# A gated convolution and mixture-of-experts block: one group's partial rows summed by accumulating DMAs, and three steps of the order moved

## The chip, the cores and the metric

One core of one Trainium2 chip. The metric is the time of one execution on the device in microseconds (us); before the change it is 213.32 us, the median of 3 runs (213.16 to 214.17). TensorE does the matrix products, VectorE, ScalarE (ACT) and GpSimd (POOL) the rest, SP issues most of the transfers.

## The reference, cut to what matters

The input is `x` (16 batches of 128 channels by 256 positions) and a context of the same shape. The first half is a gated long convolution with 16 heads of 8 channels: the products of all pairs of context channels of a head are convolved along the positions with the head's filter, multiplied with the normalised rows of `x` and summed over one of the two channel indices. The second half is a mixture of experts.

```
kv  = einsum('bhil,bhjl->bijhl', k, v)          # k = v = context
y   = irfft(rfft(kv) * rfft(ssm_kernel))[:L] + kv * D
att = einsum('bijhl,bhil->bjhl', y, layernorm(x))
x   = x + tanh(g_xattn) * att
t   = layernorm(x)
probs = softmax(t @ Wg); e = argmax(probs)      # at most 256 tokens of an expert
x   = x + tanh(g_ffn) * (gate * (silu(t @ W1[e]) * (t @ W3[e])) @ W2[e]
                         + (silu(t @ sw1) * (t @ sw3)) @ sw2)
```

All of it is fp32. The sum over `i` in the third line is what the change touches: eight products for each output row have to be added.

## The kernel before, in words

The 16 batches are worked in four groups of four (g = 0 to 3, the first to the fourth), each group in eight units of two heads, so that the convolution has 32 units or slots s = 0 to 31. From slot 16 on the feed-forward work of the shared expert is interleaved, further slots without a unit follow, and then come the eight routed experts. The order on every engine is written out by hand: `STEPS` and its exceptions `FIRST_STEPS`, `THIRD_STEPS` and `LAST_STEPS` (lines 86 to 97) place each step, and `due` (line 103) reads them: for a group g the slot is 8 (g + 1) plus the step (in the last group 32 plus the step).

One unit runs like this. GpSimd (`kv_products`, lines 503 to 511) multiplies context planes with each other, for four heads at a time, in two instructions of 768 and 128 elements per partition, and ACT makes the squares (`squares`). TensorE (`convolve`, line 1209) multiplies them with the Toeplitz matrices of the two heads into a pair of PSUM banks `z` (three places up to slot 14, then two, because the third goes to the feed-forward). VectorE (`products`, line 968, with `multiply`, line 519) multiplies the result with the turned rows `qr` in six instructions and writes eight rows of terms to the SBUF tensor `terms`, which has eight rows of 24 heads of 64 numbers (`TERMS`, `HEADS`, `TROW`); even groups use the lower 16 heads and odd groups the upper 16. An odd group works units 4 to 7 ahead of 0 to 3 (`unit`, line 122). The semaphore `prods` counts the units that VectorE has finished.

When a group has its eight units, TensorE turns and sums the terms in two halves, `turn_r(g, 0)` and `turn_r(g, 1)` (line 1249): an accumulating transpose for each row of terms, in four blocks of 128 by 128. `FULL_TERMS = 2` says that in groups 0 and 1 all eight rows are summed so, 32 transposes in a half. In groups 2 and 3 GpSimd first adds the upper four rows to the lower four, unit by unit (`fold`, line 676), and TensorE sums four rows, 16 transposes in a half. VectorE adds each half to `x_sb` (`first_residual`, line 977) and takes the statistics of the second layer norm, GpSimd raises them to the power -1/2 (`scale_and_bias`, line 645), ACT normalises into `xrow` (`norm2`), TensorE turns that (`turn_xT`), ACT copies it rounded (`xT_high`) and VectorE writes what the rounding left out (`turned_low`, the step `tokens_low`). The first feed-forward product of a group needs both (`wait_xT`, line 1275). In group 0 `turn_xT` stands in slot 15 and `tokens_low` in slot 16, ahead of VectorE's products of its slot. Slots 16 and 17 have the first two feed-forward products, 17 and 18 the halves of `turn_r(1)`, 18 and 19 its residuals, 18 the choice of experts for group 0 (`choose`), 19 the statistics of group 1, 20 `slot_of_token(0)` and `gate(0)`, 21 `turn_q` of the fourth group, 22 `turn_xT(1)`.

GpSimd's queue is one list in the order of slots (lines 697 to 725): kv products in even slots, the fold of the unit before, the scales, and the scatter of finished tokens to `xd_scratch` by indirect DMAs. SP's queue issues the loads of the start (lines 594 to 618), the third context among them.

At the start VectorE takes the statistics of the first rows (`norm_stats(0)`), makes the kv products of the first four heads itself (line 1138), normalises two of the four rows when GpSimd has the scale (line 1140), and adds the diagonals to the first Toeplitz matrices (line 1147). TensorE passes this time with two batches of 22 transposes of the identity (`turns`, line 1376, constant `TURNS`) before it turns the first rows.

Of the kernel before, what the change touches and what calls it, by code (L numbers as in the profile page):

```python
# [73 lines left out]
TERMS = 8  # L74
TURNS = 22
FULL_TERMS = 2
HEADS = 24
# [12 lines left out]
}  # L90
FIRST_STEPS = {"ln2_stats": 3, "ln2_scale": 3, "ln2_apply": 4, "turn_xT": 7, "tokens_low": 8}
THIRD_STEPS = {"ln2_apply": 4, "logits": 9, "exp": 9, "places": 10, "gate": 10, "scatter": 10}
# [29 lines left out]
def unit(s):  # L122

    g, i = divmod(s, UNITS)
    return g, (i + 4 * (g % 2)) % UNITS
# [107 lines left out]
def build(nc, x, ctxt, kpad, skip_d, g_x, g_f, wg, w1, w3, w2, sw1, sw3, sw2, out):  # L233
# [4 lines left out]
    with ExitStack() as ctx:  # L238
# [3 lines left out]
        def sem(name):  # L242
            return ctx.enter_context(nc.semaphore(name))
# [133 lines left out]
        prods = sem("prods")  # L377
        folded = sem("folded")
        expert_memory = sem("expert_memory")
        tp_ready = sem("tp_ready")  # L380
# [256 lines left out]
        def _(pool):  # L637
# [29 lines left out]
            for c in range(1, 4):  # L667
                kv_products(pool, 0, c, 1, kv_pool)
            scale_and_bias(1)
            pool.affine_select(out=tri[:, :], in_=ones[:, :], compare_op=ALU.is_ge, fill=0.0, base=-1,  # L670
# [3 lines left out]
            pool.iota(prio[:, :, :], pattern=[[0, GB], [-1, E]], base=E, channel_multiplier=0,  # L674
                      allow_small_or_imprecise_dtypes=True).then_inc(pool_consts, 1)
            def fold(s):
                g, u = unit(s)
                pool.wait_ge(prods, s + 1)
                low, high = (view(terms, first_head(g, u) * 64 + i * 4 * TROW, [[TROW, 4], [1, 128]])
                             for i in range(2))  # L680
                pool.tensor_tensor(low, low, high, ALU.add).then_inc(folded, 1)  # L681

            def scatter(g, parts):
# [12 lines left out]

            for s in range(SLOTS):
                g, i = kv_due(s)
                if g >= 0:
                    kv_place_free(pool, g, i)  # L700
                    kv_products(pool, g, i, 1, kv_pool)
                if 1 <= s <= CONV and unit(s - 1)[0] >= FULL_TERMS:
                    fold(s - 1)
# [228 lines left out]
        def _(dve):  # L932
# [203 lines left out]
            norm_stats(0)  # L1136
            dve.wait_ge(ctx_first, 16)
            kv_products(dve, 0, 0, 0, kv_dve)
            dve.wait_ge(rstd_done, 1)
            for b in range(2, GB):  # L1140
                ins = dve.tensor_scalar(xn[:, b, :], x_sb[:, b, :], rstd[:, b:b + 1], nbias[:, b:b + 1], ALU.mult, ALU.add)
            ins.then_inc(xn_dve, 1)
            dve.wait_ge(anti_turned, 1)
            dve.wait_ge(d_in, 1)
# [63 lines left out]
        def _(pe):  # L1208
# [40 lines left out]
            def turn_r(g, k):  # L1249
                pe.wait_ge(prods, UNITS * (g + 1))  # L1250
                if g >= FULL_TERMS:
                    pe.wait_ge(folded, UNITS * (g + 1 - FULL_TERMS))
                n = TP_AT[("r", g, k)]
                tp_wait(pe, n)
                for j in range(2 * BLK):
                    b, blk = 2 * k + j // BLK, j % BLK
                    for t in range(terms_of(g)):
                        src = view(terms, t * TROW + first_head(g, 0) * 64 + blk * GB + b, [[PL, CH]])
                        mm = pe.matmul(tp[n % 2][:, j * P:(j + 1) * P], src, ident[:, :], is_transpose=True,  # L1259
                                       start=(t == 0), stop=(t == terms_of(g) - 1))  # L1260
                mm.then_inc(tp_ready, 1)
# [121 lines left out]
            pe.matmul(fb[1][:, 0:2], ones[0:H, :], d_of[:, :], start=True, stop=True).then_inc(spread, 1)  # L1383
            turns(TURNS)
            turn_q(0)
# [55 lines left out]
```

## Time and profile before

| | |
|---|---|
| median of 3 runs | 213.32 us (213.16 to 214.17) |
| the profiled execution's own time | 213.18 us |
| its span, first to last instruction | 211.4 us, 4244 instructions |
| TensorE busy | 198.2 us, 94% |
| VectorE busy | 157.2 us, 74% |
| GpSimd busy | 125.5 us, 59% |
| ACT busy | 92.0 us, 44% |
| granted clock of TensorE, mean | 0.995 |

Times are counted from the span's start; 1.8 us of the execution lie around the span. A row of a timeline gives start, duration, engine, line, operation, tensors and count, and in brackets for how long the engine had been idle and what ended that. A row with a count (xN) merges neighbours and starts with the first of them. Neighbouring instructions of one engine overlap by some 0.1 us in their records.

### The profile page before, as it was taken

How to read it: one execution, taken by the hardware profiler on the slowest of the kernel's cores; microseconds unless marked ns; L12 is line 12 of the kernel's file. 1: busy time of each engine (PE TensorE's matmuls, PEld its weight loads, DVE VectorE, ACT ScalarE, POOL GpSimd, SP SyncE). 2: the span in 40 equal slices, each digit the busy share in tenths (PEclk: the TensorE clock that was granted, in tenths of full speed). 3: DMA queues.
4: the chain of work that ended last, by engine and by line, in shares of the span. 5: the costliest groups of instructions: out<-in, count | busy, mean ns of one | idle time of the engine just before them, and what ended most of it. 6: DMA issues, size and time to landing. Idle time of an engine off the chain costs nothing.

```text
span 211.4 us, 4244 instructions
## 1 busy us (share of the span) xinstructions
PE 198.2 (94%) x1441; PEld 184.5 (87%) x1441; DVE 157.2 (74%) x512; ACT 92.0 (44%) x184; POOL 125.5 (59%) x135
## 2 busy tenths in 40 slices
PE   5999899997999999999999998999999999999960
PEld 5986799886998899898989998999999999999950
DVE  5749894997789976589868877776767995878530
ACT  2252744291163732232347248645374445724300
POOL 4695999395836499604682262460072687677661
PEclk9999999999999999999999999999999999999998
DMA  5799995000000010010201899744638679422221
GB/s 159 211 344 357 322 398 222 0 3 0 5 0 0 0 53 25 28 51 0 100 3 50 264 351 364 273 132 130 190 86 257 200 236 327 134 79 71 67 92 50
DMA packets 21497, 29.77 MB, mean 141 GB/s; under 512 B 2834, under 2 KB 18970, under 8 KB 21476
## 3 DMA queue, kind: packets, MB, share of 16 engines
q1 hardware_dynamic: 18960, 23.24, 33.5%
q0 software_dynamic: 2304, 6.05, 8.8%
q8 instruction: 11, 0.18, 0.4%
q10 hardware_dynamic: 212, 0.22, 0.3%
q14 instruction: 10, 0.08, 0.1%
HBM read 21.32 MB, written 8.45 MB: 141 GB/s over the span
## 4 chain that ended last, share of the span: by engine, by line
PE 76%; POOL 7%; DVE 7%; issue 5%; ACT 2%; POOLq 1%; ACTq 0%; DVEq 0%
PE fbz L1324 16%; PE z L1324 14%; PE z L1234 7%; PE tp L1259 7%; PE z L1345 6%; PE z L1359 5%; DVE terms L527 4%; PE z L1231 4%; PE fbz L1359 4%; POOL kv L508 4%; PE tp L1378 3%; PE fbz L1345 2%; PE tp L1370 2%; PE tp L1271 1%; POOL kv L511 1%
## 5 line engine op out<-in xcount | busy, mean ns | idle before, releaser
L527 DVE TENSOR_TENSOR terms<-z,qr 128x512 f32<-128x512 f32 (+1 forms) x162 | 41.4, 326 | 8.1 <-PE z L1234 8.1
L1234 PE MATMUL z<-kv,toep 128*128 128x288 f32 x108 | 35.0, 406 | 0.0
L1324 PE MATMUL fbz<-xTh,wh_gu 128*128 128x256 f32 (+1 forms) x104 | 31.7, 305 | 1.6 <-issue 1.6
L735 POOL DMA_INDIRECT kv<-out,tok x16 | 20.3, 1271 | 16.3 <-DMA out<-x_sb 11.7
L508 POOL TENSOR_TENSOR kv<-ct 128x768 f32<-128x768 f32 x15 | 27.5, 1834 | 3.8 <-PE z L1234 3.3
L1324 PE MATMUL fbz<-xTl,wh_gu 128*128 128x256 f32 (+1 forms) x104 | 29.0, 279 | 0.0
L1324 PE MATMUL fbz<-xTh,wl_gu 128*128 128x256 f32 (+1 forms) x104 | 29.0, 279 | 0.0
L681 POOL TENSOR_TENSOR terms<-terms 128x512 f32<-128x512 f32 x16 | 20.2, 1282 | 11.8 <-DVE terms L527 11.8
L686 POOL DMA_INDIRECT xd_scratch<-xrow,dest x16 | 16.7, 1046 | 17.1 <-DVE xrow L1029 7.3
L1324 PE MATMUL z<-xTh,wh_gu 128*128 128x256 f32 (+1 forms) x88 | 25.3, 287 | 0.0
L1324 PE MATMUL z<-xTl,wh_gu 128*128 128x256 f32 (+1 forms) x88 | 24.5, 278 | 0.0
L1324 PE MATMUL z<-xTh,wl_gu 128*128 128x256 f32 (+1 forms) x88 | 24.4, 278 | 0.0
L746 POOL DMA_INDIRECT out<-kv,tok x16 | 16.1, 1005 | 13.2 <-DVE hL L1053 9.7
L1259 PE MATMUL tp<-ident,terms 128*128 128x128 f32 x192 | 22.9, 277 | 0.0
L1259 PEld LDWEIGHTS tp<-ident,terms 128*128 128x128 f32 x192 | 22.2, 193 | 0.3
L1231 PE MATMUL z<-kv,toep 128*128 128x144 f32 x108 | 22.4, 289 | 0.0
L1231 PEld LDWEIGHTS z<-kv,toep 128*128 128x128 f32 x108 | 19.0, 190 | 3.9 <-issue 0.2
L1324 PEld LDWEIGHTS fbz<-xTh,wh_gu 128*128 128x128 f32 (+1 forms) x104 | 19.3, 185 | 3.0 <-issue 2.4
L1324 PEld LDWEIGHTS fbz<-xTh,wl_gu 128*128 128x128 f32 (+1 forms) x104 | 19.3, 186 | 0.5
L825 ACT ACTIVATE sg<-fbz 128x256 f32<-128x256 f32 (+1 forms) x26 | 9.7, 374 | 22.3 <-PE fbz L1324 22.2
L1324 PEld LDWEIGHTS fbz<-xTl,wh_gu 128*128 128x128 f32 (+1 forms) x104 | 19.2, 185 | 0.0
L653 POOL TENSOR_TENSOR rstd<-veps,mhalf 128x4 f32<-128x4 f32 x8 | 9.2, 1146 | 14.6 <-DVE mneg L956 14.6
(164 smaller groups left out, 450.2 us busy)
## 6 DMA issues: line engine op xcount, KB each, us to landing
terms<-w SPq DMA_DIRECT2D x16, 352.0 KB, 4.3
ct<-ctxt SPq DMA_DIRECT2D x3, 768.0 KB, 8.5
xd_scratch<-xrow SPq DMA_DIRECT2D x4, 516.0 KB, 8.9
kv<-xd_scratch SPq DMA_DIRECT2D x8, 258.0 KB, 4.0
out<-x_sb SPq DMA_DIRECT2D x8, 256.0 KB, 2.4
terms<-w SPq DMA_DIRECT2D x8, 256.0 KB, 4.9
toep<-kskip_scratch SPq DMA_DIRECT2D x3, 512.0 KB, 8.7
x_sb<-x SPq DMA_DIRECT2D x3, 512.0 KB, 6.3
```

The costliest lines, as they stand in the source:

```text
L508: eng.tensor_tensor(dst, left, right, ALU.mult)
L527: return eng.tensor_tensor(view(terms, t0 + row * TROW + col, [[64, 2], *td]), view(src, zo, [[512, 2], *zd]), view(qr, q0 + qo, [[CW, 2], ...
L681: pool.tensor_tensor(low, low, high, ALU.add).then_inc(folded, 1)
L686: pool.indirect_dma_start(out=xd, out_offset=bass.IndirectOffsetOnAxis(ap=dest[:, n:n + 1], axis=0), in_=xrow[:, g % 2, b, :], in_offset=N ...
L735: pool.indirect_dma_start(out=bg[:, e % BRING, t, :], out_offset=None, in_=out_rows, in_offset=bass.IndirectOffsetOnAxis(ap=tok[:, e, t:t ...
L746: pool.indirect_dma_start(out=out_rows, out_offset=bass.IndirectOffsetOnAxis(ap=tok[:, e, t:t + 1], axis=0), in_=fin[:, e % 2, t, :], in_o ...
L1231: pe.matmul(view(zs, k * 512 + GB, [[PL, NPL], [1, GB]]), toep[:, h, P:2 * P], view(kv, o, [[PL, NPL], [1, GB]]), start=True, stop=False, ...
L1234: mm = pe.matmul(zs[:, k, 0:KVH], toep[:, h, 0:P], view(kv, o, [[1, KVH]]), start=False, stop=True, skip_group_check=True)
L1259: mm = pe.matmul(tp[n % 2][:, j * P:(j + 1) * P], src, ident[:, :], is_transpose=True, start=(t == 0), stop=(t == terms_of(g) - 1))
L1324: mm = pe.matmul(bank[0:rows(blk, c), m * 256:(m + 1) * 256], wt[w % 2][:, col:col + rows(blk, c)], xt[:, place, k, first:first + 256], st ...
L1345: mm = pe.matmul(bank[:, t * L:(t + 1) * L], rounded_hidden(blk, c, h_low)[0:rows(blk, c), t * P:(t + 1) * P], rounded_down(blk, d_low, c ...
L1359: mm = pe.matmul(bank[:, t * L:(t + 1) * L], hidden(blk, c)[0:rows(blk, c), t * P:(t + 1) * P], down[0:rows(blk, c), c * L:(c + 1) * L], s ...
```

## The change

Six edits.

1. VectorE normalises its two first rows ahead of its kv products of the first four heads, in place of behind them.
2. TensorE's second batch of identity transposes has 13 in place of 22.
3. GpSimd makes three constants (`tri`, `ebase`, `prio`) ahead of the scale of the second group's rows, in place of behind it.
4. The step `tokens_low` of group 0 stands in slot 15 in place of 16.
5. Group 1's eight rows of terms are summed to four before TensorE turns them (`FULL_TERMS = 1`), so each half of `turn_r(1)` has 16 transposes in place of 32. Seven of its eight units are summed by two accumulating DMAs that GpSimd issues (`sum_rows`): one over four units, in slot 12, once products(11) are done (128 partitions, 4 rows of 512 numbers, 1,048,576 bytes written), and one over three units, in slot 15, once products(14) are done (4 rows of 384 numbers, 786,432 bytes). The eighth, unit 15, is folded by GpSimd as in the later groups, at the head of slot 16, ahead of that slot's kv products.
6. `turn_r` of every group from 1 on waits for both DMAs and for the folds.

```diff
-TURNS = 22
-FULL_TERMS = 2
+TURNS, TURNS_BEHIND = 22, 13
+FULL_TERMS = 1
+SUMS = {4: (0, 4), 7: (4, 3)}
+SUMMED = 7
...
-FIRST_STEPS = {"ln2_stats": 3, "ln2_scale": 3, "ln2_apply": 4, "turn_xT": 7, "tokens_low": 8}
+FIRST_STEPS = {"ln2_stats": 3, "ln2_scale": 3, "ln2_apply": 4, "turn_xT": 7, "tokens_low": 7}
...
             for c in range(1, 4):
                 kv_products(pool, 0, c, 1, kv_pool)
-            scale_and_bias(1)
...
             pool.iota(prio[:, :, :], pattern=[[0, GB], [-1, E]], base=E, channel_multiplier=0,
                       allow_small_or_imprecise_dtypes=True).then_inc(pool_consts, 1)
+            scale_and_bias(1)
...
+            def sum_rows(g, first, n):
+                pool.wait_ge(prods, UNITS * g + first + n)
+                low, high = (view(terms, first_head(g, unit(UNITS * g + first)[1]) * 64 + i * 4 * TROW,
+                                  [[TROW, 4], [1, 128 * n]]) for i in range(2))
+                pool.dma_start(low, high, accum_op=ALU.add).then_inc(summed, 16)
...
             for s in range(SLOTS):
+                if s - UNITS in SUMS:
+                    sum_rows(1, *SUMS[s - UNITS])
+                if s == UNITS + SUMMED + 1:
+                    fold(s - 1)
                 g, i = kv_due(s)
                 if g >= 0:
                     kv_place_free(pool, g, i)
                     kv_products(pool, g, i, 1, kv_pool)
-                if 1 <= s <= CONV and unit(s - 1)[0] >= FULL_TERMS:
+                if UNITS + SUMMED + 1 < s <= CONV:
                     fold(s - 1)
...
             norm_stats(0)
-            dve.wait_ge(ctx_first, 16)
-            kv_products(dve, 0, 0, 0, kv_dve)
             dve.wait_ge(rstd_done, 1)
             for b in range(2, GB):
                 ins = dve.tensor_scalar(xn[:, b, :], x_sb[:, b, :], rstd[:, b:b + 1], nbias[:, b:b + 1], ALU.mult, ALU.add)
             ins.then_inc(xn_dve, 1)
+            dve.wait_ge(ctx_first, 16)
+            kv_products(dve, 0, 0, 0, kv_dve)
...
             def turn_r(g, k):
                 pe.wait_ge(prods, UNITS * (g + 1))
                 if g >= FULL_TERMS:
-                    pe.wait_ge(folded, UNITS * (g + 1 - FULL_TERMS))
+                    pe.wait_ge(summed, 16 * len(SUMS))
+                    pe.wait_ge(folded, UNITS * g - SUMMED)
...
-            turns(TURNS)
+            turns(TURNS_BEHIND)
             turn_q(0)
             convolve(0)
```

## Rows read from the trace of the kernel before

**Rows 1.** The page: busy times, then granted clock and DMA rate in 40 slices.

```profile
PE 198.2 (94%) x1441; PEld 184.5 (87%) x1441; DVE 157.2 (74%) x512; ACT 92.0 (44%) x184; POOL 125.5 (59%) x135
...
PEclk9999999999999999999999999999999999999998
...
GB/s 159 211 344 357 322 398 222 0 3 0 5 0 0 0 53 25 28 51 0 100 3 50 264 351 364 273 132 130 190 86 257 200 236 327 134 79 71 67 92 50
```

**Rows 2.** The chain of waits in order of time: start, us, engine, tensor, line.

```profile
54.13 3.58 PE tp L1259 x32
...
59.51 3.79 PE tp L1259 x32
...
71.94 2.08 ACT xrow L758 x4
```

**Rows 3.** Timeline of ACT and TensorE around slots 15 and 16.

```profile
46.40 1.08 ACT L802 ACTIVATE xTh<-tp 128x512 fp32r<-128x512 f32 x2
...
49.63 0.36 PE L1324 MATMUL fbz<-xTh,wh_gu 128*128 128x256 f32 x1 [1.36 <-issue]
```

**Rows 4.** Timeline of VectorE, slots 15 to 20.

```profile
46.80 1.53 DVE L527 TENSOR_TENSOR terms<-z,qr 128x512 f32<-128x512 f32 x6
48.25 1.28 DVE L1097 TENSOR_TENSOR xTl<-tp,xTh 128x512 fp32r<-128x512 f32 x2
49.45 1.53 DVE L527 TENSOR_TENSOR terms<-z,qr 128x512 f32<-128x512 f32 x6
51.96 0.42 DVE L1053 TENSOR_TENSOR hL<-fbz,sg 128x256 f32<-128x256 f32 x1 [0.98 <-ACT sg L825]
52.75 1.54 DVE L527 TENSOR_TENSOR terms<-z,qr 128x512 f32<-128x512 f32 x6 [0.36 <-PE z L1234]
54.83 0.42 DVE L1053 TENSOR_TENSOR hL<-fbz,sg 128x256 f32<-128x256 f32 x1 [0.54 <-ACT sg L825]
...
57.75 0.75 DVE L984 SCALAR_TENSOR_TENSOR x_sb<-tp,tg,x_sb 128x512 f32<-128x512 f32 x1 [0.76 <-PE tp L1259]
59.26 1.54 DVE L527 TENSOR_TENSOR terms<-z,qr 128x512 f32<-128x512 f32 x6 [0.77 <-PE z L1234]
...
64.86 1.55 DVE L527 TENSOR_TENSOR terms<-z,qr 128x512 f32<-128x512 f32 x6 [0.34 <-PE z L1234]
66.32 1.40 DVE L947 BATCH_NORM_STATS2 stats<-x_sb 128x6 f32<-128x256 f32 x4
```

**Rows 5.** Timeline of GpSimd, slots 12 to 17.

```profile
42.38 1.83 POOL L508 TENSOR_TENSOR kv<-ct 128x768 f32<-128x768 f32 x1
...
46.80 1.81 POOL L508 TENSOR_TENSOR kv<-ct 128x768 f32<-128x768 f32 x1
...
51.06 1.27 POOL L681 TENSOR_TENSOR terms<-terms 128x512 f32<-128x512 f32 x1 [2.03 <-DVE terms L527]
```

**Rows 6.** The scatter by its source line: durations, idle before, time to landing.

```profile
L686 POOL DMA_INDIRECT xd_scratch<-xrow,dest x16: 968/984/1666, 72.3 to 138.5; - x16
...
  issue: 3.2, 11
...
DMA to landing us min/median/max: 2.4/2.8/7.0
```

**Rows 7.** Timeline of the head, and the power by its source line.

```profile
6.50 1.23 DVE L508 TENSOR_TENSOR kv<-ct 128x1024 f32<-128x1024 f32 x1
6.65 1.94 POOL L653 TENSOR_TENSOR rstd<-veps,mhalf 128x4 f32<-128x4 f32 x1 [3.35 <-DVE mneg L956]
...
L653 POOL TENSOR_TENSOR rstd<-veps,mhalf x8: 1011/1038/1944, 6.7 to 118.8; 128x4 f32<-128x4 f32 x8
```

**Rows 8.** Timeline of ACT, GpSimd and VectorE around the third context's landing.

```profile
29.32 0.42 ACT L779 ACTIVATE kv<-ct 128x256 f32<-128x256 f32 x1 [4.12 <-DMA ct<-ctxt]
29.37 1.86 POOL L508 TENSOR_TENSOR kv<-ct 128x768 f32<-128x768 f32 x1
...
35.87 0.75 DVE L1157 BATCH_NORM_STATS2 stats<-x_sb 128x6 f32<-128x256 f32 x2 [2.37 <-POOL nbias L654]
```

More of the change, by code:

```diff
@@ L378, in build @@
         folded = sem("folded")
+        summed = sem("summed")
         expert_memory = sem("expert_memory")
```

## The prediction

> **What bounds the kernel now.** I read the page first: TensorE's granted clock is at its upper level (2.4 GHz) in all but the last slice, so the clock is no term here, and VectorE is busy 74% of the span [rows 1]. That average hides the stage that matters, so the chain of waits comes next, in order of time. From 49.6 us on it lies almost wholly on TensorE, and two of its longest pieces are the second group's transposing sums (`turn_r`, L1259): 32 transposes in 3.58 us and 32 in 3.79 us [rows 2]. The third and fourth group, whose terms GpSimd has folded, have 16 in each. The same view shows ACT's `xrow` normalisation before the second `turn_xT`, 71.94 to 74.02: the chain leaves TensorE there [rows 2]. Then the timelines. TensorE idles 1.36 us before the first feed-forward product (slot 16) [rows 3]; what it waits for is VectorE's `tokens_low`, 48.25 to 49.53, which stands behind the products of unit 15 [rows 4]. VectorE has short gaps from 51 to 65 us, 0.98, 0.36, 0.54, 0.76, 0.77 and 0.34, 3.75 us in all, and none from then to 66.32 [rows 4]. So in slots 16 to 19 TensorE sets the pace, but VectorE is only 3.75 us short of setting it.
>
> **Tokens split a unit sooner.** The two subtractions of `tokens_low(0)` (1.28 us) go ahead of products(15). They need ACT's copies, which end at 46.40 + 1.08 = 47.48; products(14) end where products(15) start now, at 46.8 [rows 3, 4]. The pair then ends at about 48.25, VectorE having idled some 0.13 us; the products of 15 and 16 follow, the latter ending at 51.1 in place of 50.98. TensorE's feed-forward starts at 48.35 instead of 49.63: 1.28 us sooner, and it reaches `turn_r(1,0)` at 54.13 - 1.28 = 52.85. What is queued behind the new wait on VectorE is products(15), ending 49.8; unit 17 needs its bank just then, when the feed-forward ends. Nothing is lost on TensorE.
>
> **Half the transposes.** 32 of the 64 go, (3.58 + 3.79)/2 = 3.7 us by their own rows (half of each piece; 16 are 1.79 us by the first) [rows 2]. With the 1.28 that is 5.0 us on TensorE. VectorE can't follow that far. Of its 3.75 us of gaps some 0.5 stays (the second feed-forward's sigmoid arrives 1.28 sooner, 53.55, VectorE is there at 53.05), and 0.13 was spent above: 3.1 us is what slots 16 to 19 can shrink by [rows 4]. From products(19) on, unit 21, its feed-forward, `turn_q`, ACT's copies, the `xrow` step and `turn_xT` hang on each other, and each moves by the same 3.1 us; behind them TensorE is dense to the end, and stores, expert loads and scatters are released by the work that moves.
>
> **The sums on GpSimd and the DMA queue.** No accumulating DMA and no plain GpSimd DMA is in this trace, so both prices are bounded. For the issue the nearest row is the scatter: 0.98 us of GpSimd for 128 rows, 0.30 between two (3.2/11), 1.28 together [rows 6]. Lower end 0.4 (a mere start), upper end 3.9 (four times 0.98, since a sum has 512 rows): I take 1.28. GpSimd is ready for the first sum at 42.38 and products(11) end at 42.5; it then makes both kv products (to 46.80 in the trace before, 4.42 for the two) [rows 5]. So the second sum starts at 46.80 + 0.1 + 1.28 = 48.2; its own wait, products(14), is over by then. Behind it stand `fold(15)`, kv(3,0), `fold(16)`, and so on, about 4 us later than now; kv(3,0) is for unit 24 and the third group's folds for 84 us, and GpSimd has idle stretches before both, so I cost that at nothing. If each issue is 3.9 us instead, the second sum itself comes late: the slow rival below. The one fold that is added, for unit 15, is another 1.28 on GpSimd [rows 5], hidden likewise.
>
> For the transfer: the scatter (132,096 B) lands 2.4 us after its start at best [rows 6]; at the 398 GB/s of the fastest slice [rows 1] its bytes take 0.33, so 2.07 is fixed. The second sum writes 786,432 B. Lower end, the bytes once: 1.98, landed after 4.05. Each written element needs two operands read, which is twice the bytes: 3.95, landed after 6.02; I take this, because the source and the destination both have to come out of SBUF. Upper end, two reads and a write in turn: 5.93, landed after 8.0. The first sum (1 MB) lands at 42.5 + 2.07 + 5.27 = 49.8 and isn't late; the DMA rows are empty there [rows 1].
>
> So the second lands at 54.2. What does waiting cost? products(18) started 59.26 - 57.71 = 1.55 us after `turn_r(1,0)` ended [rows 2, 4]. With the chain 1.28 earlier and the gaps of 0.76 and 0.77 gone VectorE could start them at 59.26 - 1.28 - 1.53 = 56.45, so the transposes must start by 56.45 - 1.55 - 1.79 = 53.1. At 54.25 they cost 1.15 us. Break-even is 53.1 + 3.1 = 56.2, that is 8.0 us after the second sum's start.
>
> By the Trainium skill, DMA: Bandwidth & Descriptors, Anatomy of one DMA, a GpSimd DMA takes about 2.0 us plus its bytes at 436 GB/s; an estimate from that page is 3.8 us, landing at 52.0 with no wait, and the whole 3.1 us stays. The Trainium skill's Collectives: The Full Stack, The bandwidth ceiling, speaks against the change: an add in the DMA engine reads two sources, so it moves half of what a copy does. By the first page the time is 210.2, by the second about 211.4; no row here shows either.
>
> **The head.** VectorE's kv product (6.50 on) ran beside GpSimd's power, which took 1.94 us where the median of eight is 1.04 [rows 7]. With the product behind xn the power has VectorE out of its way and I expect the first rows some 0.9 us sooner; the product then starts near 8.7 instead of 6.50, the diagonal behind it, so conv(0) gains only about 0.3 to 0.4 and products(0) with it. Nine fewer turns, at 3.58/32 = 0.11 each [rows 2], take 1.0 us off the cover in front of `turn_q(0)`. If the power stays at 1.94, conv(0) is 0.6 late. Either is hidden: kv(2,0) starts on GpSimd at 29.37, when the transfer of the third context has landed (ACT waited 4.12 us for it, to 29.32), GpSimd runs on from there to the ln1 scale, and VectorE waits 2.37 us for that until 35.87 [rows 8]. The three small constants moved ahead on GpSimd vanish in the same way. I cost all of it at 0.0; both ends are within 0.1, since GpSimd's arrival and the landing lie 0.05 apart.
>
> **The sum**: -3.1 + 1.15 = -1.95 us. The profiled execution took 213.18, which gives 211.2; it lies 0.14 under the median of 213.32, so I forecast **211.4**. Within 0.5% (1.07 us) a measurement of this kernel can't tell it from no change.
>
> **Rivals.** *A, the sum lands unseen* (at or before 53.1): 3.1 us, 210.2. For it: an empty DMA system, and a copy's rate suffices. Against: two operands. 0.25. *B, TensorE gets its whole 5.0 us*: 208.3. VectorE would have to work through what it has no gaps for: 0.04. *C, three passes*: landing at 56.2, cost 3.1, no gain, 213.3; DMA work and waits are merely exchanged. 0.18. *D, slower*: descriptors cost GpSimd 0.98 us per 128 rows. Each sum then holds it for 3.9 us, the second issue runs from 50.8 to 54.7, and the end of the transfer comes 1.4 (2.4 - 0.98) plus half of its 3.95 behind: 58.1. `turn_r(1,0)` waits to 58.1, cost 5.0, net +1.9: 215.2. It decides from a landing at 57.3 on. For it: four times the rows of a scatter; against: nothing shows that the scatter's 0.98 grows with its rows. 0.15. That the head decides is a part of none: its cover is 2.4 us deep.
>
> **How the numbers follow.** Forecast 0.38, A 0.25, B 0.04, C 0.18, D 0.15. Faster by over 0.5%: the forecast, A and B, 0.67. Within: 0.18. Slower: 0.15. The range leaves out B's end and most of D: 209.4 (between A and B) to 214.2 (C with 0.9 more).
>
> **What would show it.** The feed-forward of slot 16 follows conv(16) with no 1.3 us idle; L1259 counts 160; GpSimd's two new rows last about 1 us; `turn_r(1,0)` starts near 54.2, released by a DMA on `terms`; VectorE has at most two gaps from 51 to 64 us; the second `turn_xT` starts near 72.1; VectorE's row at 35.87 hasn't moved. An issue row of over 2 us, or a landing over 8 us after it, proves the forecast wrong, and so does a TensorE wait on GpSimd's folds in the third group.

## The result and the profile after

The changed kernel takes 218.68 us (median of 6; 216.74 to 220.55) where the kernel before, beside it, takes 213.75 (213.16 to 214.49): ratio 1.0203, interval 1.0154 to 1.0251. The forecast was 211.4, in a range of 209.4 to 214.2: the sign is wrong and the range missed. The executions fall into two lots, near 217 and near 220 us; the one profiled here, 220.28 (span 218.5), is of the upper lot, and one of the lower lot is read at the run e9_after_again.

The page, with the lines of [rows 1] and the queue of GpSimd's DMAs:

```profile
PE 198.9 (91%) x1400; PEld 184.3 (84%) x1400; DVE 158.8 (73%) x512; ACT 91.7 (42%) x184; POOL 128.9 (59%) x138
...
PEclk9999999999679699999999999999999999999998
...
GB/s 165 211 360 327 307 405 172 0 139 179 22 0 3 0 48 3 48 7 43 51 48 24 105 341 366 332 199 146 94 149 175 206 298 270 168 98 72 65 89 48
...
q0 software_dynamic: 3360, 7.88, 13.5%
```

TensorE issues 1400 instructions in place of 1441 (41 fewer: 32 transposes and 9 turns), and is busy for 0.7 us longer. The granted clock, 9s throughout before, has 6 and 7 in the two slices from 54.6 to 65.5 us and 6 in the one from 71.0 to 76.5, and the DMA row shows the sums at 139 and 179 GB/s where [rows 1] has 3 and 0. The queue carries 1056 packets more than before (2304).

The chain of waits, in order of time, answers to [rows 2]:

```profile
48.56 1.61 PE fbz L1338 x12
...
57.06 3.65 PE tp L1273 x16
...
67.41 1.70 DVE acc L1029
...
80.93 1.09 PE tp L1285 x8
```

The feed-forward of slot 16 starts at 48.56 in place of 49.63, so the tokens did their part. The first 16 transposes start at 57.06, later than the 32 did (54.13), and last 3.65 us where 32 took 3.58. At 67.41 a step of VectorE's choosing of experts stands in the chain for 1.70 us. `turn_xT(1)` runs at 80.93 against 74.05 before: 6.9 us late, and the span is 7.1 longer. So all of the loss is made between 54 and 81 us.

GpSimd's timeline there ([rows 5] of before), and its DMAs by their source line:

```profile
43.02 1.59 POOL L690 DMA_DIRECT2D terms<-terms  x1 [0.41 <-DVE terms L530]
...
48.50 1.85 POOL L690 DMA_DIRECT2D terms<-terms  x1
...
65.05 1.27 POOL L684 TENSOR_TENSOR terms<-terms 128x512 f32<-128x512 f32 x1 [4.67 <-DVE terms L530]
67.27 1.81 POOL L511 TENSOR_TENSOR kv<-ct 128x768 f32<-128x768 f32 x1 [0.95 <-PE z L1247]
```

```profile
L690 POOL DMA_DIRECT2D terms<-terms x2: 1587/1720/1852, 43.0 to 48.5; - x2
...
DMA to landing us min/median/max: 8.5/8.5/8.5
```

The issues take 1.59 and 1.85 us, and each sum lands 8.5 us after its start: the second at 57.0, where TensorE's wait ends. GpSimd isn't behind with its work: it had idled 4.67 us before the fold of 65.05, which VectorE's products of unit 18 released, and 0.95 before the kv product of 67.27, which a convolution released. What follows on TensorE is seen in the windows (behind a stretch and its length stand busy time and instructions of PE, PEld, DVE, ACT and POOL, then the granted clock, the DMA share and GB/s):

```profile
51.00:53.00 2.00, 2.00 (x17) 1.86 (x15) 1.90 (x9) 0.16 (x1) 2.00 (x2) 1.00 1.14 186
53.00:55.00 2.00, 0.17 (x2) 0.00 (x0) 1.47 (x8) 0.94 (x3) 2.00 (x4) 1.00 1.14 184
55.00:57.00 2.00, 0.00 (x0) 0.00 (x0) 0.99 (x6) 0.00 (x0) 2.00 (x4) 0.78 0.16 27
57.00:59.00 2.00, 1.94 (x9) 1.97 (x10) 0.00 (x0) 0.00 (x0) 1.83 (x4) 0.50 0.00 0
...
61.00:63.00 2.00, 2.00 (x7) 1.47 (x6) 0.50 (x1) 1.98 (x5) 0.00 (x0) 0.52 0.00 0
```

The busy share of the DMA engines is 1.14, at 184 to 186 GB/s, until 55. TensorE has nothing to do from 53.2 to 57.06, and its granted clock falls: 0.78 in the stretch 55 to 57, 0.50 (1.2 GHz) from 57 on to 0.52 in the stretch that ends at 63, while the transposes run. They take 3.65 us; in the execution of e9_after_again, whose clock stays up there, they take 2.02. VectorE behind them, answering to [rows 4]:

```profile
60.75 0.75 DVE L997 SCALAR_TENSOR_TENSOR x_sb<-tp,tg,x_sb 128x512 f32<-128x512 f32 x1 [4.72 <-PE tp L1273]
63.43 1.55 DVE L530 TENSOR_TENSOR terms<-z,qr 128x512 f32<-128x512 f32 x6 [1.93 <-PE z L1247]
...
65.33 1.03 DVE L1017 SCALAR_TENSOR_TENSOR t<-sh,prio 128x32 f32<-128x32 f32 x1
...
67.41 1.70 DVE L1029 TENSOR_TENSOR acc<-acc,oh 128x8 f32<-128x8 f32 x1
```

The residual waits 4.72 us (0.76 before), the products of unit 18 another 1.93 (0.77). Then two steps on 32 and 8 numbers per partition take 1.03 and 1.70 us, while their neighbours take 0.19. GpSimd's fold at 65.05 and its kv product at 67.27 run just then (the fence above). The steps choose from 64.89 to 69.43. In the kernel before the fold was there already, and the kv product was not, since it came behind the last step of choosing (63.55 to 63.74):

```profile
61.17 1.04 DVE L1004 SCALAR_TENSOR_TENSOR t<-sh,prio 128x32 f32<-128x32 f32 x1
...
64.91 1.83 POOL L508 TENSOR_TENSOR kv<-ct 128x768 f32<-128x768 f32 x1 [2.75 <-PE z L1234]
```

Both times the product waits for the convolution of unit 19. That is done 2.4 us after choosing begins here and 4.2 us after it before (60.73), because the second half of `turn_r(1)`, which stands in front of it on TensorE, now has 16 transposes.

The head, [rows 7], and VectorE's row behind the ln1 scale, [rows 8]:

```profile
6.66 1.01 POOL L656 TENSOR_TENSOR rstd<-veps,mhalf 128x4 f32<-128x4 f32 x1 [3.34 <-DVE mneg L969]
...
12.46 1.55 DVE L530 TENSOR_TENSOR terms<-z,qr 128x512 f32<-128x512 f32 x6 [1.88 <-PE z L1247]
...
13.09 0.48 PE L1244 MATMUL z<-kv,toep 128*128 128x144 f32 x2 [0.36 <-DMA toep<-kskip_scratch]
```

```profile
36.04 0.75 DVE L1170 BATCH_NORM_STATS2 stats<-x_sb 128x6 f32<-128x256 f32 x2 [2.52 <-POOL nbias L657]
```

The power is down to 1.01 us and products(0) start 0.4 sooner, but the next convolution waits for a DMA on `toep`, and VectorE's row after the ln1 scale is at 36.04 (35.87 before): nothing is left of it.

### The profile page after: what moved, and what is told of

Read it like the earlier page. It is cut to its first block, busy times and chain, and to the rows that moved or that the text cites. A ratio compares the mean times of both kernels' runs of the same rounds, so it can differ in the third digit from the quotient of the medians.

```text
span 218.5 us, 4171 instructions
## 1 busy us (share of the span) xinstructions
PE 198.9 (91%) x1400; PEld 184.3 (84%) x1400; DVE 158.8 (73%) x512; ACT 91.7 (42%) x184; POOL 128.9 (59%) x138
## 4 chain that ended last, share of the span: by engine, by line
PE 76%; DVE 9%; DMA 5%; issue 4%; ACT 2%; POOL 1%; POOLq 1%; ACTq 0%; DVEq 0%
PE fbz L1338 14%; PE z L1338 14%; PE z L1247 9%; PE tp L1273 8%; PE z L1359 6%; PE z L1244 5%; PE z L1373 5%; DVE terms L530 4%; PE fbz L1373 4%; DMA toep<-kskip_scratch 3%; PE fbz L1359 2%; PE tp L1285 2%; PE tp L1384 2%; PE fbz L1247 1%; DMA dcol<-skip_d 1%
## 5 line engine op out<-in xcount | busy, mean ns | idle before, releaser
L1247 PE MATMUL z<-kv,toep 128*128 128x288 f32 x108 | 36.1, 417 | 0.0
L1338 PE MATMUL fbz<-xTh,wh_gu 128*128 128x256 f32 (+1 forms) x104 | 32.5, 312 | 0.4 <-issue 0.4
L684 POOL TENSOR_TENSOR terms<-terms 128x512 f32<-128x512 f32 x17 | 22.6, 1345 | 16.5 <-DVE terms L530 16.4
L511 POOL TENSOR_TENSOR kv<-ct 128x768 f32<-128x768 f32 x15 | 29.5, 1976 | 3.2 <-DMA ct<-ctxt 2.3
L1338 PE MATMUL fbz<-xTl,wh_gu 128*128 128x256 f32 (+1 forms) x104 | 29.6, 284 | 0.0
L1244 PE MATMUL z<-kv,toep 128*128 128x144 f32 x108 | 23.1, 296 | 3.5 <-DVE terms L530 3.0
L1244 PEld LDWEIGHTS z<-kv,toep 128*128 128x128 f32 x108 | 19.4, 195 | 8.0 <-issue 4.3
L1273 PE MATMUL tp<-ident,terms 128*128 128x128 f32 x160 | 21.0, 292 | 3.9 <-issue 3.9
L1273 PEld LDWEIGHTS tp<-ident,terms 128*128 128x128 f32 x160 | 20.0, 196 | 4.3 <-issue 4.1
L1338 PEld LDWEIGHTS fbz<-xTl,wh_gu 128*128 128x128 f32 (+1 forms) x104 | 19.9, 191 | 0.0
L1247 PEld LDWEIGHTS z<-kv,toep 128*128 128x128 f32 x108 | 17.4, 195 | 0.0
```

Source lines behind the costliest of these rows:

```text
L511: eng.tensor_tensor(dst, left, right, ALU.mult)
L1244: pe.matmul(view(zs, k * 512 + GB, [[PL, NPL], [1, GB]]), toep[:, h, P:2 * P], view(kv, o, [[PL, NPL], [1, GB]]), start=True, stop=False, ...
L1247: mm = pe.matmul(zs[:, k, 0:KVH], toep[:, h, 0:P], view(kv, o, [[1, KVH]]), start=False, stop=True, skip_group_check=True)
L1338: mm = pe.matmul(bank[0:rows(blk, c), m * 256:(m + 1) * 256], wt[w % 2][:, col:col + rows(blk, c)], xt[:, place, k, first:first + 256], st ...
```

## The experiments

Theory after the result: the late landing of the second sum (57.0 instead of 54.2) is the whole loss. The fall of the clock came in with e5 as a cost of its own, and GpSimd's blocking of VectorE with e7 and e8. Each ratio is to the kernel before on the same chip.

**e1_tokens.** The kernel before with edit 4 alone.

```diff
-FIRST_STEPS = {"ln2_stats": 3, "ln2_scale": 3, "ln2_apply": 4, "turn_xT": 7, "tokens_low": 8}
+FIRST_STEPS = {"ln2_stats": 3, "ln2_scale": 3, "ln2_apply": 4, "turn_xT": 7, "tokens_low": 7}
```

> The kernel before with one edit: tokens_low of group 0 in slot 15. Theory (the edit itself is good, the loss of the whole change comes from the second accumulating DMA): TensorE's idle of 1.36 us in front of the slot 16 feed-forward goes, VectorE absorbs it in its gaps, so 1.0 to 1.3 us faster than before, clock at its upper level throughout. Rival (the edit puts VectorE's wait for ACT's copies ahead of products(15) and delays the units behind it): 0 to 1 us slower than before, with a gap of VectorE of over 0.3 us ahead of L1097.

Ratio 0.9934 [0.991, 0.9958], 1.4 us faster. Timelines of TensorE and VectorE:

```profile
53.02 3.77 PE L1259 MATMUL tp<-ident,terms 128*128 128x128 f32 x32
...
60.25 1.04 DVE L1004 SCALAR_TENSOR_TENSOR t<-sh,prio 128x32 f32<-128x32 f32 x1
```

TensorE's feed-forward starts at 48.56 in place of 49.63, and the 32 transposes 0.95 us sooner (53.97 before, by the same view). A choose step of 1.04 us stands here too: it ran beside the fold at 59.97, and the kernel before has the same (1.04 at 61.17 beside a fold at 60.89). I had not read that row.

**e2_head.** The kernel before with edits 1 to 3 alone.

```diff
             norm_stats(0)
-            dve.wait_ge(ctx_first, 16)
-            kv_products(dve, 0, 0, 0, kv_dve)
...
+            dve.wait_ge(ctx_first, 16)
+            kv_products(dve, 0, 0, 0, kv_dve)
```

> The kernel before with the three edits of the head: rows ahead of the kv products on VectorE, 13 in place of 22 turns, constants ahead of the scale on GpSimd. Theory (hidden behind the landing of the third context): the power takes 1.0 in place of 1.94 us, units 0 starts 0.3 to 0.5 sooner, VectorE's row behind the ln1 scale still starts at 35.9, time within 0.3 us of before. Rival (the head costs part of the 5 us): 0.5 to 1.5 us slower, the row at 35.9 late by as much.

Ratio 0.9984 [0.9945, 1.0024]: the head moves nothing.

**e3_no_sums.** The changed kernel without its two DMAs; the upper four rows of terms of seven of eight units are left out of the result. It gives the edit's value if the sum were free.

```diff
-                if s - UNITS in SUMS:
-                    sum_rows(1, *SUMS[s - UNITS])
...
-                    pe.wait_ge(summed, 16 * len(SUMS))
```

> The changed kernel without its two accumulating DMAs and the waits on them; it leaves out the upper four rows of seven of eight units of group 1, all else is the changed kernel. Theory (the DMAs' landing is the whole loss): turn_r(1,0) starts at 52.9 to 53.4, the granted clock stays at its upper level, 3.1 us faster than before and about 7 to 8 us faster than the changed kernel's profiled run. Rival 1 (VectorE isn't a bound): 5.0 us faster than before. Rival 2 (folds and kv products on GpSimd cost too): under 1.5 us faster than before.

Ratio 0.9823 [0.977, 0.9876]: 3.8 us faster than before. Timelines:

```profile
58.47 0.19 DVE L1015 SCALAR_TENSOR_TENSOR t<-sh,prio 128x32 f32<-128x32 f32 x1
...
59.89 1.27 POOL L684 TENSOR_TENSOR terms<-terms 128x512 f32<-128x512 f32 x1
...
52.87 1.97 PE L1270 MATMUL tp<-ident,terms 128*128 128x128 f32 x16
```

The transposes start at 52.87 (53.03 in the chain of waits, by which 52.85 was forecast), and choosing takes 2.2 us (58.03 to 60.2): VectorE is early, GpSimd is still at its scale and starts the fold only at 59.89, behind the steps that it held before. The step of 1.04 us is back at 0.19, 0.85 us less, and with the 3.1 of gain that I had worked out this makes 3.95, near the measured 3.8.

**e4_copies.** The same two DMAs without the addition (the lower rows are overwritten by the upper).

```diff
-                pool.dma_start(low, high, accum_op=ALU.add).then_inc(summed, 16)
+                pool.dma_start(low, high).then_inc(summed, 16)
```

> The changed kernel with plain copies of the same bytes in place of the two accumulating DMAs; it leaves the addition out (the upper rows replace the lower ones). Theory (the accumulation is slow in the DMA engines, some 178 GB/s by the DMA rows from 45 to 55 us): a copy runs at twice that or more, the second lands 4 to 5.5 us after its start (8.5 when accumulating), turn_r(1,0) starts by 54, the clock doesn't fall, 2 to 3.1 us faster than before. Rival (GpSimd's DMA path or rows of 2 KB in SBUF are slow whatever is done with them): landing again after 8 us or more, and a loss like that of the change.

Ratio 0.982 [0.9785, 0.9854]. The DMAs by their line, and one window while the first runs:

```profile
L690 POOL DMA_DIRECT2D terms<-terms x2: 804/916/1028, 43.1 to 48.5; - x2
...
DMA to landing us min/median/max: 4.0/4.5/5.1
```

```profile
45.00:47.00 2.00, 2.00 (x16) 1.74 (x15) 2.00 (x10) 1.84 (x5) 2.00 (x3) 1.00 1.01 377
```

The same bytes, unadded, move at 377 GB/s and land after 4.0 to 5.1 us in place of 8.5, with half the issue time; the whole gain of e3 is there. What makes the sum late is the addition, not the DMA.

**e5_filler.** The changed kernel with 36 more identity transposes on TensorE ahead of the wait, to keep it busy.

```diff
+                if g == 1 and k == 0:
+                    n = TP_AT[("r", g, k)]
+                    tp_wait(pe, n)
+                    for _ in range(FILL):
+                        pe.transpose(tp[n % 2][:, 0:P], ident[:, :], ident[:, :])
```

> The changed kernel with 36 transposes of the identity (about 4 us at the upper clock) on TensorE in place of its idle time, in front of the wait for the sums; the wait itself stays. Theory (the loss has two parts, the wait of about 4 us and the fall of the clock behind it, which made 16 transposes take 3.65 in place of 1.8 us and the two convolutions of unit 18 about 1.3 us longer): turn_r(1,0) again starts near 57, the clock stays at its upper level, its 16 transposes take 1.8 to 2.0 us, and the whole is 2.5 to 4 us faster than the changed kernel, so 213.5 to 215.5. Rival (the idle time alone is the loss, the clock's fall is hidden behind VectorE): within 1 us of the changed kernel.

Ratio 1.022 [1.0165, 1.0275], the rival's number; 217.73 to 218.99 us in 4 executions. Timelines:

```profile
53.56 4.09 PE L1269 MATMUL tp<-ident 128*128 128x128 f32 x36
57.63 2.06 PE L1279 MATMUL tp<-ident,terms 128*128 128x128 f32 x16
...
69.77 0.82 PE L1245 MATMUL z<-kv,toep 128*128 128x144 f32 x2 [3.00 <-DVE terms L531]
...
65.22 1.70 DVE L1030 TENSOR_TENSOR acc<-acc,oh 128x8 f32<-128x8 f32 x1
```

The clock stays up through the filler and the transposes take 2.06 us, and none of the four executions lies near 220. But the median is hardly better: choosing is still blocked (1.70 at 65.22), TensorE then idles 3.00 us, and there the clock falls instead (matmul pairs of 0.82 us where 0.41 to 0.48 is usual). So taking the first fall away moves the fall on and gains nothing that can be measured.

**e6_second_alone.** The first DMA is left out, and with it the upper rows of the first four units.

```diff
-SUMS = {4: (0, 4), 7: (4, 3)}
+SUMS = {7: (4, 3)}
```

> The changed kernel with the second accumulating DMA alone; it leaves out the upper rows of the first four units of group 1. Both theories have the rate of 178 GB/s of the addition. Theory (rate and queue: the second waited for the first one's last bytes): alone it lands 2.6 + 4.4 = 7.0 us after its start, near 55.5, so some 1.5 us of the 8.5 was queueing. Rival (each accumulating DMA takes 8.5 us, whatever its size, as both did): 8.5 again.

One execution, 214.84 us. The landing by the source line:

```profile
DMA to landing us min/median/max: 7.3/7.3/7.3
```

Alone, the second sum lands after 7.3 us (forecast 7.0) and moves at 184 to 185 GB/s. Of the 1.2 us to the 8.5 little is queueing. In windows of 0.5 us its bytes begin some 2.2 us after its start in both kernels; they end at about 55.1 here and 55.2 in the changed kernel, and the landing follows 0.8 us later here (55.9) and 1.8 us later there (57.0). In e9 and e13, with the first sum ahead, the second landed after 7.7 and 7.8 us. What makes up the last microsecond stays open.

**e7_one_sum.** Only the first sum by DMA; GpSimd folds units 12 to 15, its kv(2,3) moves behind them.

```diff
-SUMS = {4: (0, 4), 7: (4, 3)}
-SUMMED = 7
+SUMS = {4: (0, 4)}
+SUMMED = 4
...
+                if s == 16:
+                    fold(15)
+                    kv_step(2, 3)
+                if kv_due(s)[0] >= 0 and s != 14:
+                    kv_step(*kv_due(s))
```

> The changed kernel with the first accumulating DMA alone (units 8 to 11), which lands at 51.5, and GpSimd folding units 12 to 15, with its kv products for units 22 and 23 moved behind the last fold and the scale of slot 18 ahead of kv products. The output is whole. Theory: the last fold ends near 51.5, turn_r(1,0) starts at 53.0, no fall of the clock, 3.1 to 3.9 us faster than before, 209.6 to 210.4. Rival (GpSimd is now the bound, its folds and kv products come late): a wait of TensorE for folded or kv, under 2 us faster than before.

Ratio 1.0052 [1.0019, 1.0084]. The transposes are on time (53.02, at the upper clock), as in the theory, and still there is no gain; nor does TensorE wait for a fold or for kv, as in the rival. The timelines of GpSimd, VectorE and TensorE tell why:

```profile
59.34 1.81 POOL L511 TENSOR_TENSOR kv<-ct 128x768 f32<-128x768 f32 x1
59.37 1.81 DVE L1032 TENSOR_TENSOR pair<-oh 128x8 f32<-128x8 f32 x1
...
65.66 0.58 PE L1251 MATMUL z<-kv,toep 128*128 128x144 f32 x1 [3.29 <-DVE terms L530]
```

`pair` adds two columns of 8 and takes 1.81 us, exactly as long as the GpSimd product that had started 0.03 us ahead of it. TensorE then idles 3.29 us, and behind that its clock falls (0.61 in the stretch 65 to 67).

**e8_all_folds.** No DMA; GpSimd folds all eight units, its kv(2,2) and kv(2,3) move behind them.

```diff
-SUMMED = 7
+SUMMED = 0
...
+                if s == 12:
+                    for k in range(9, 12):
+                        fold(k)
```

> No accumulating DMA at all: GpSimd folds all eight units of group 1, in its idle time from 39 us on and with two kv products moved behind the last fold. The output is whole. Theory: the last fold ends at 51 to 52, as with one sum, 3 to 3.9 us faster than before; the DMA wasn't needed. Rival (VectorE and GpSimd block each other where both read two SBUF tensors, and the scale of group 0 comes late behind a fold): 1 us or more slower than with one sum.

Ratio 0.9938 [0.9909, 0.9967], no better than e1's and neither the theory's nor the rival's. The transposes are at 52.64, but a VectorE step on 4 numbers, `mneg`, took 1.85 us beside a kv product of GpSimd's (65.29, 1.81 us):

```profile
65.27 1.85 DVE L981 TENSOR_SCALAR mneg<-mv 128x4 f32<-128x4 f32 x1
```

It has one input in SBUF only. TensorE idles 2.29 us some steps behind it, and its clock falls to 0.50 from 68.75 on.

**e9_after_again.** The changed kernel unedited, on the chip of e10 to e12.

> The changed kernel unchanged, beside the next three on one chip. Its six runs so far lay at 216.7 to 217.5 and at 219.9 to 220.5. Theory (the near or far side is how long VectorE's small steps of choose are blocked by GpSimd's instructions and how long the clock is down): a run on the near side, if profiled, has a shorter stretch at the lower clock or shorter blocked steps than the 1.03 and 1.70 us of the profile at hand. Rival (something of the whole chip, not of this kernel): every engine's rows are longer throughout.

Ratio 1.0236 [1.0192, 1.028]; 216.91 to 222.28. The profiled execution took 216.91:

```profile
55.46 2.02 PE L1273 MATMUL tp<-ident,terms 128*128 128x128 f32 x16 [2.65 <-issue]
...
60.51 0.18 DVE L1014 TENSOR_REDUCE mx<-tp 128x4 f32<-128x32 f32 x1
...
62.89 1.82 POOL L511 TENSOR_TENSOR kv<-ct 128x768 f32<-128x768 f32 x1 [0.95 <-PE z L1247]
...
63.03 1.71 DVE L1029 TENSOR_TENSOR acc<-acc,oh 128x8 f32<-128x8 f32 x1
...
67.57 0.48 PE L1244 MATMUL z<-kv,toep 128*128 128x144 f32 x2 [3.00 <-DVE terms L530]
```

The second sum landed after 7.7 us, the wait is 2.65 us here and the clock stays at 1.00 behind it; 16 transposes take 2.02. The transposes start 1.6 us before those of the execution of 220.28 (57.06), choosing starts 4.4 us before (64.89): by this pair of profiles 2.8 us is what the clock's fall at the first wait costs. The blocked steps are no shorter (1.05 and 1.71 us), and TensorE idles the same 3.00 us behind them; its clock falls there (0.80 in the stretch 67 to 69, 0.50 in 69 to 71).

**e10_one_sum_apart, e11_folds_apart.** e7 and e8 with a gate in slot 18: GpSimd starts the kv product of that slot and its folds from unit 17 on only when VectorE has done group 1's last residual, so that they don't fall into choosing.

```diff
+                if s in (18, 20):
+                    scales()
+                if s == 18:
+                    pool.wait_ge(tp_free_dve, sum(not BY_ACT[k[0]] for k in TP[:TP_AT[("r", 1, 1)] + 1]))
```

> As with one sum (e7), but GpSimd issues no kv product or fold until the residual behind choose is done, and makes the scale of slot 20 ahead of its kv product. The output is whole. Theory (in e7 the transposes were on time at 53.0, as without sums, and what ate the gain were GpSimd's kv product and folds that ran beside choose and blocked VectorE's steps with two SBUF inputs for 1.81 and 1.12 us, then a TensorE idle of 3.3 us and its clock): choose takes 2.2 in place of 5.0 us, the clock stays up, 3 to 3.9 us faster than before. Rival (choose is slow for another reason, GpSimd's delay only adds): no faster than e7, 214 or more.

> As with all folds on GpSimd (e8) and the same gate in front of choose. The output is whole. Theory: choose takes 2.2 us, and with GpSimd's queue later than in e10 the folds of the third group may come late: 1.5 to 3.5 us faster than before. Rival (choose isn't what is slow): within 0.5 us of e8.

Ratios 0.9907 [0.9877, 0.9938] (e7: 1.0052) and 0.9894 [0.9866, 0.9922] (e8: 0.9938); e10 gains 2.0 us, less than the theory's 3 to 3.9. In e10 every choose step is 0.16 to 0.19 us, in e11 all but one, of 0.56 beside the end of a fold. A new wait stands behind, on TensorE in e10:

```profile
82.83 2.03 PE L1282 MATMUL tp<-ident,terms 128*128 128x128 f32 x16 [1.46 <-POOL terms L684]
```

The third group's folds are late, since GpSimd waited. In e11 `turn_xT(1)` ran at 70.45, as in e3 (70.27), but the third group's transposes at 81.56 against 79.83.

**e12_filler_apart.** e5 with the gate (at slot 19).

```diff
+                if s == 19:
+                    pool.wait_ge(tp_free_dve, sum(not BY_ACT[k[0]] for k in TP[:TP_AT[("r", 1, 1)] + 1]))
```

> The changed kernel with the filler of e5 and with GpSimd kept off choose. It removes both followers of the late sum and leaves the wait itself. Theory (loss of the changed kernel = wait of about 4 us beyond VectorE's slack + clock + 2.3 us of blocking in choose): 2 to 4 us faster than e5, so 213.8 to 215.8. Rival (choose only moves the idle time): within 1 us of e5's 217.9.

Ratio 0.9998 [0.9966, 1.003], against 1.022 without the gate: 4.8 us, more than the 2 to 4 of the theory. Timelines:

```profile
63.17 0.17 DVE L1032 TENSOR_TENSOR acc<-acc,oh 128x8 f32<-128x8 f32 x1
...
66.17 0.48 PE L1247 MATMUL z<-kv,toep 128*128 128x144 f32 x2 [0.61 <-DVE terms L531]
```

Choosing takes 2.2 us in place of 4.55, TensorE idles 0.61 in place of 3.00 and keeps its clock; `turn_xT(1)` runs at 73.66 against 78.68. Of these 5.0 us 1.1 was there before the transposes, 2.35 is choosing, and the remaining 1.5 lies behind it, where e5 has the idle stretch and the lower clock.

**e13_after_apart.** The changed kernel with that gate and nothing else.

> The changed kernel, with GpSimd held before its fold of row 18 until VectorE's last step of choosing for group 1's second half is done; no filler. Theory (the clock is a cost of its own): the wait for the second sum, some 3.9 us on the changed kernel's page, again lets TensorE's granted clock fall to 0.50 over the 16 transposes, which take some 3.65 us instead of 1.96, so choosing starts about 1.7 us later than with filler; the choose steps take 0.18 to 0.19 us each. The time is 1.5 to 3 us above that of the filler kernel with the same gate (ratio 0.9998 there), so a ratio of 1.007 to 1.014, and 2 to 4 us below the changed kernel. Rival (the clock's cost is hidden behind other waits once GpSimd is out of the way): a ratio within 0.004 of 1.000.

Ratio 1.0006 [0.9969, 1.0042]: the rival's number. Timelines:

```profile
58.04 2.02 PE L1275 MATMUL tp<-ident,terms 128*128 128x128 f32 x16 [3.24 <-issue]
...
63.52 0.19 DVE L1019 SCALAR_TENSOR_TENSOR t<-sh,prio 128x32 f32<-128x32 f32 x1
```

TensorE idled 3.24 us here, the second sum landing at 57.96, and its clock stayed up. So the one edit on GpSimd takes away the whole loss, with the wait for the sum still there. What the clock costs this execution can't show. The mean granted clock on record is 0.971 to 0.979 in five of the twelve executions, which average 215.3 us, and 0.983 to 0.992 in the other seven, which average 214.4: with the gate it still falls in some, and then costs about 1 us in place of the theory's 1.5 to 3.

**e14_folds_first, e15_one_sum_first.** e11 and e10 with kv(3,3) behind the fold of unit 23 (the diff is e14's).

```diff
-                if kv_due(s)[0] >= 0 and s not in (12, 14):
+                if kv_due(s)[0] >= 0 and s not in (12, 14, 22):
...
+                if s == 24:
+                    kv_step(3, 3)
```

> All eight folds of group 1 on GpSimd, no sum by DMA, the gate of e11_folds_apart, and the product kv(3,3) moved behind the fold of row 23. Theory (in e11 the third group's transposes wait some 1.3 to 1.8 us for GpSimd's folds, which run behind that product): turn_r(2,0) starts near 79.8 instead of 81.56 us, and the time falls by 1 to 1.8 us below e11's ratio of 0.9894, to about 0.981 to 0.985. Rival (the wait only moves to the product itself, which PE or VectorE then needs): the ratio stays within 0.003 of 0.989.

> The kernel e10_one_sum_apart (the first sum by DMA alone, gate before the fold of row 18) with the same move of kv(3,3) behind the fold of row 23. Theory: PE's transposes of the third group's first half, which stood at 82.83 us released by GpSimd's folds, start 1.8 to 2.4 us sooner, ratio about 0.980 to 0.984 against 0.9907. Rival: the product is then late and the ratio stays within 0.003 of 0.991.

Ratios 0.9855 [0.9803, 0.9907] and 0.9832 [0.979, 0.9874], at the edge of the theory's band and in it. Timelines of e14:

```profile
74.83 5.00 POOL L684 TENSOR_TENSOR terms<-terms 128x512 f32<-128x512 f32 x4
79.77 1.86 POOL L511 TENSOR_TENSOR kv<-ct 128x768 f32<-128x768 f32 x1
...
80.54 1.96 PE L1288 MATMUL tp<-ident,terms 128*128 128x128 f32 x16
```

The four folds run in one piece and the product behind them; the third group's transposes start at 80.54 (81.56 in e11, 79.82 in e15, 79.83 in e3) and wait for nothing. e15 is the best version that leaves nothing out: 210.93 us against 214.41, 3.5 us, within 0.001 of the ratio of e3. One small step is still held in both: `xrow`, on 4 numbers, takes 1.65 and 1.64 us beside a kv product, where it takes 0.23 before.

## Why the prediction was wrong

**Right:** the tokens (e1: 1.4 us, worked out 1.28), the start of the transposes if nothing is late (52.85 against 53.03), the head at nothing (e2), the issue (I took 1.28; GpSimd's next instruction starts 1.09 and 1.51 us after the two issues do), and nearly the size of the gain: 3.1 against e3's 3.8, where a block of 0.85 in choosing goes as well.

**The transfer was mis-sized, and this alone takes the gain away.** "Landed after 6.02" was 8.5. The bytes were nearly right: the two reads at 398 GB/s, 3.95 us, are 786,432 B at 184 GB/s (e6), 4.27. Wrong was "so 2.07 is fixed", which came from the scatter: it is 7.3 - 4.27 = 3.0 us alone and 8.5 - 4.27 = 4.2 in the changed kernel. The start was 48.50 for 48.2. With the landing at 57.0 the working's own rule gives a cost of 1.15 + 2.8 = 3.95 and a net of +0.85, some 214.2; minus the 0.85 that choosing gains once GpSimd is held, no change. That is what e12 and e13 measure (0.9998, 1.0006). Rival C had nearly this landing (56.2) and this result by luck: its three passes would have taken 5.93 us, and the bytes took 4.27. The Trainium skill's estimate by the page DMA: Bandwidth & Descriptors, Anatomy of one DMA (3.8 us), fits e4's copy of the second sum's bytes (4.0) and not the addition; the rule of Collectives: The Full Stack, The bandwidth ceiling, half of a copy's rate, agrees: 184 against 377 GB/s.

**The step that gave the loss was "GpSimd has idle stretches before both, so I cost that at nothing".** It asked who waits for GpSimd's folds and products, not whom they stop while they run. GpSimd's lateness did cost nothing, since it had idled 4.67 us again before its fold. But the late sum makes products(18) late, these release the fold just when choosing begins, and the halved `turn_r(1,1)` brings the convolution of unit 19 forward, which releases the kv product into choosing: 4.5 us in place of 3.0, in the executions of 220.28 and 216.91 alike. The idle time of TensorE that follows is 3.00 us, and its clock falls there, in the execution of 220.28 at the first wait too. Together these are what lies between 1.0203 to 1.0236 and 1.000 to 1.0006: 2.0 to 2.4%, or 4.2 to 5.1 us on the mean; single executions of the changed kernel lie 2.1 (216.91) to 7.4 us (222.28) above the median of the kernel before. That they go by a gate on GpSimd alone is shown by e13 against e9, and by e12 against e5. How much of it is the block and how much the clock is read from pairs of profiles only (e5 and e12: 2.35 and 1.5 us; e9 and the changed kernel: 2.8 for a fall at the first wait), not shown by a run of its own, and why the clock falls in some executions stays open.

The evidence stood in the trace of before: GpSimd's power of 1.94 beside VectorE's product [rows 7], on which my own argument for the head rested, and the choose step of 1.04 us. The Trainium skill, SBUF — State Buffer, SBUF: two separate sides, states it: a VectorE operation with two inputs in SBUF, or in a mode that uses two ports, and a GpSimd operation exclude each other for the whole instruction. The runs agree (1.81 and 1.81 in e7). They also agree in that VectorE's products, with `z` in PSUM, are not held by folds: in e3 the six of 49.69 took 1.54 us beside the fold of 49.85. Steps with one input are held as well (`mneg` in e8); whether in such a mode no run shows. The page doesn't fit GpSimd's power on 4 numbers: in e3 it ran from 58.60 to 59.64, and the choose steps with two inputs in SBUF beside it took 0.16 to 0.19 us.

**"The clock is no term here"** was true of the kernel before alone. A wait that is added can take it away: behind the first wait 16 transposes took 3.65 in place of 2.02 us. The slow rival, D, had the sign and not the cause, which is luck: it asked for an issue of 3.9 us, and the issues take 1.59 and 1.85.

## What to carry to other kernels

Before GpSimd's work is moved, or what releases it, list which small VectorE instructions with inputs in SBUF lie where it will now run: on the critical path they were held here until the large GpSimd instruction ended, and a gate that makes GpSimd wait was worth 4.2 to 5.1 us. Cost an adding DMA at half of a copy's rate, and take what is added to its bytes' time from an adding DMA too (3.0 to 4.2 us here, where a small scatter gave 2.07). And when a wait is added ahead of TensorE, price it at both clocks.

## What the runs showed of the hardware

- A DMA that adds SBUF to SBUF moved 184 to 186 GB/s of written bytes in full flow, a copy of the same tiles 377; 768 KB landed 7.3 us after its start alone (e6) and 7.7 to 8.5 with 1 MB ahead of it, 1 MB 8.5 or 9.4 us after its start (9.4 in e7 and e12), and the issue took 1.59 to 1.86 us on GpSimd against 0.80 to 1.03 for the copy.
- TensorE's granted clock fell from 1.00 to its lower level, 0.50, behind idle stretches of 3.89 us (the changed kernel), 3.29 (e7), 3.00 (the changed kernel, e5, e9) and 2.29 (e8), and stayed at 1.00 behind 3.24 (e13), 3.02 (e6) and 2.65 (e9): the length of the idle stretch alone doesn't say which.
- VectorE's steps on 4 to 32 numbers per partition took 1.03 to 1.85 us where a GpSimd fold or product held them, and 0.15 to 0.24 otherwise.
